# Expert weights fetched early by the sync engine, their high and low parts made in halves, one per tile

## The reference

```python
x = x + 0.5 * ffn(layernorm(x), Wg, W11, W12, W2)
x = x + attn(layernorm(x), ...)      # conv, two linear recurrences, gate
x = x + 0.5 * ffn(layernorm(x), Wg, W11, W12, W2)

def ffn(x, Wg, W11, W12, W2):        # 8 experts, the best 2 of each row
    scores = softmax(x @ Wg); top, idx = top_k(scores, 2); top /= top.sum() + 1e-8
    gate, value = x @ W11[e], x @ W12[e]            # 256 -> 512
    out_e = (gate * sigmoid(gate) * value) @ W2[e]  # 512 -> 256
    return sum of top * out_e over the two chosen e
```

## Time and profile before

| what | value |
|---|---|
| median of three runs | 1039.33 us |
| profiled execution | 1031.17 us, span 1029.4 us |
| PE busy | 919.6 us, 89% of the span |
| DVE, ACT, POOL busy | 600.6, 330.0, 602.4 us |
| round 0, first matmul of tile 0 to first matmul of tile 70 | 84.21 to 445.52 us |
| round 1, the same | 668.21 to 1008.30 us |
| DMA queues | q0 (POOL) 37.83 MB, q1 (SP) 49.82 MB, q10 (ACT) 23.61 MB |

### The profile page before, as it was taken

One profiled execution on the slowest core, in us unless ns is written; L12 is line 12 of the kernel. 1 busy time (PEld: TensorE's weight loads), 2 busy tenths in 40 slices (PEclk: granted clock), 3 DMA queues, 4 the chain that ended last, 5 costly groups with the idle time before them and its releaser, 6 DMA issues.

```text
span 1029.4 us, 20399 instructions
## 1 busy us (share of the span) xinstructions
PE 919.6 (89%) x5412; PEld 794.1 (77%) x5413; DVE 600.6 (58%) x1478; ACT 330.0 (32%) x655; POOL 602.4 (59%) x549
## 2 busy tenths in 40 slices
PE   7957999999999999984997995399999999999995
PEld 6945878888888888873775684388888888888884
DVE  5486656656556465536766885855555555555552
ACT  3431333424334332221226541023233223322321
POOL 4104766767667677743214770157777777777773
PEclk9999999999999999997999996599999999999998
DMA  9435466464573754323212547234344343343332
GB/s 345 141 103 185 77 173 159 81 191 108 139 190 57 195 131 92 57 27 108 62 41 61 185 143 317 89 87 73 58 78 68 57 78 55 72 76 58 52 49 30
DMA packets 75970, 111.86 MB, mean 109 GB/s; under 512 B 11792, under 2 KB 60816, under 8 KB 75600
## 3 DMA queue, kind: packets, MB, share of 16 engines
q0 software_dynamic: 31808, 37.83, 23.8%
q1 hardware_dynamic: 31744, 49.82, 14.3%
q10 hardware_dynamic: 12368, 23.61, 6.6%
HBM read 66.79 MB, written 48.63 MB: 112 GB/s over the span
## 4 chain that ended last, share of the span: by engine, by line
PE 66%; DVE 12%; DMA 6%; issue 5%; POOL 4%; ACTq 3%; ACT 3%; POOLq 0%; DVEq 0%; SPq 0%
PE bank L1254 34%; PE bank L1277 16%; PE bank L1263 5%; PE bank L1246 3%; DMA x_rows<-yb,idx_i 3%; PE bank L1182 2%; PE bank L1371 2%; DVE work L787 2%; DMA xn_rows<-work 1%; DVE bnst L775 1%; POOL seq L438 1%; DVE sg L947 1%; DVE work L861 1%; ACT sg L617 1%; DVE w_lo L1019 1%
## 5 line engine op out<-in xcount | busy, mean ns | idle before, releaser
L947 DVE TENSOR_TENSOR sg<-sg,bank 128x512 f32<-128x512 f32 x142 | 97.7, 688 | 303.3 <-ACT sg L617 303.3
L1254 PE MATMUL bank<-w_hi,xt_hi 128*128 x568 | 241.8, 426 | 17.8 <-DVE xt_lo L936 15.9
L1254 PE MATMUL bank<-w_hi,xt_lo 128*128 x568 | 225.3, 397 | 0.0
L1254 PE MATMUL bank<-w_lo,xt_hi 128*128 x568 | 223.6, 394 | 0.0
L449 POOL DMA_INDIRECT xg<-xn_rows,idx_i x142 | 144.3, 1016 | 116.4 <-DVE idx_i L875 73.8
L609 ACT ACTIVATE yb<-bank,gates_in 128x256 f32<-128x256 f32 x142 | 67.3, 474 | 448.6 <-DMA out_rows<-yb,idx_i 216.6
L453 POOL DMA_INDIRECT gates_in<-gate_rows,idx_g x142 | 136.4, 961 | 52.0 <-issue 41.7
L1277 PE MATMUL bank<-w_hi,ft_hi 128*128 x568 | 159.4, 281 | 7.2 <-ACT yb L609 7.2
L462 POOL DMA_INDIRECT x_rows<-yb,idx_i x71 | 115.4, 1626 | 77.1 <-DMA x_rows<-yb,idx_i 36.1
L1277 PE MATMUL bank<-w_hi,ft_lo 128*128 x568 | 160.1, 282 | 0.0
L1277 PE MATMUL bank<-w_lo,ft_hi 128*128 x568 | 159.9, 282 | 0.0
(11 more groups left out here) (209 smaller groups left out, 1249.5 us busy)
## 6 DMA issues: line engine op xcount, KB each, us to landing
xn_rows<-work SPq DMA_DIRECT2D x16, 512.0 KB, 2.8
w_lo_rows<-w_lo ACTq DMA_DIRECT2D x16, 512.0 KB
w_lo<-w_lo_rows SPq DMA_DIRECT2D x16, 512.0 KB
work<-x_rows SPq DMA_DIRECT2D x16, 512.0 KB, 3.7
w_lo<-w_lo_rows SPq DMA_DIRECT2D x2, 4096.0 KB, 17.8
x_all<-x SPq DMA_DIRECT2D x8, 512.0 KB, 8.2
w_lo_rows<-in_sb ACTq DMA_DIRECT2D x16, 256.0 KB, 2.4
out_rows<-seq SPq DMA_DIRECT2D x8, 512.0 KB, 3.3
```

The source lines that it names most:

```text
L947: nc.vector.tensor_tensor(sg[p], sg[p], ps_g[p][:], ALU.mult).then_inc(f_step, 1)
L1254: last = nc.tensor.matmul(dst[p][:], xt[p][:, c, :], of(w), start=(c == 0 and n == 0), stop=(c == DC - 1 and n == len(parts) - 1))
```

## The change

Four things change, all in round 0.

1. The loads of slots 1 to 7 leave ACT. SP issues them, one slot as soon as `ye_done` is at j+1, that is, behind `down(0)` for slot 1, behind `down(1)` for slot 2, up to `down(6)` for slot 7. W2 is loaded straight into its place in `w2_hi`, in one DMA of 512 KB.
2. ACT makes the high parts in pieces of 512 columns, one for each of the steps s = 1 to 6. For W2 a piece takes two instructions: raw values to `w2_stage`, a wait for that, and the rounded copy back.
3. DVE makes the low parts in pieces of 512 columns, at s = 2 to 7.
4. ACT stores only the low part of W2, in one DMA at s = 0 of the next group; the low parts of W11 and W12 are stored by SP, slot 0 behind the last load, slot j behind the load of W2's low part of slot j.

```diff
+        def load_down(q, j, e):
+            q.dma_start(w2_hi[:, j * IC:(j + 1) * IC, :].bitcast(F32), w2[...]...).then_inc(w2_in[j], 16)
+        def load_slot(q, j):
+            e = expert_of_slot(q, j)
+            load_up(q, j, e)
+            load_down(q, j, e)
...
             store_gates(0)
-            load_w2_lo(0)
+            load_w2_lo(0, 0)
+            for j in range(1, E):
+                sp.wait_ge(ye_done, j + 1)
+                load_slot(sp, j)
+            store_up_lo(0)
+            for j in range(1, E):
+                load_w2_lo(0, j)
+                store_up_lo(j)
+            sp.wait_ge(w2_lo_in, E * 16)
...
+            def high_up(j, c):
+                act.wait_ge(w11_in[j], 16)
+                nc.scalar.activation(w11_hi[:, j * DC + c, :], w11_raw[:, j * DC + c, :], ACT.Copy).then_inc(hi11_ready, 1)
...
+            def high_down(j, h):
+                at_ = w2_hi[:, j * IC + 2 * h:j * IC + 2 * h + 2, :].rearrange("p c d -> p (c d)")
+                act.wait_ge(w2_in[j], 16)
+                if j > 0:
+                    act.wait_ge(w2_lo_out, 16 * j)
+                nc.scalar.activation(w2_stage[h], at_.bitcast(F32), ACT.Copy).then_inc(staged, 1)
+                act.wait_ge(staged, 2 * j + h + 1)
+                nc.scalar.activation(at_, w2_stage[h], ACT.Copy).then_inc(hi2_ready, 1)
...
             def weights_step(t):
                 j, s = t // MIN_TILES + 1, t % MIN_TILES
                 if t == 0:
                     store_low(0)
                 if j < E:
-                    if s == 0:
-                        load_up(act, j, expert_of_slot(act, j))
-                    if s == 1:
-                        for h in range(2):
-                            act.wait_ge(w2_lo_out[h], 16 * j)
-                        load_down(act, expert_of_slot(act, j))
-                    if s == 3:
-                        high_up(j)
-                    if s == 4:
-                        high_value(j)
-                    if s == 5:
-                        high_down(j)
-                    if s == 7:
-                        store_low(j)
+                    if s in (1, 2):
+                        high_up(j, s - 1)
+                    if s in (3, 4):
+                        high_value(j, s - 3)
+                    if s in (5, 6):
+                        high_down(j, s - 5)
+                if s == 0 and 2 <= j <= E:
+                    store_low(j - 1)
...
@@ VectorE, weights_step @@
-                    if s == 4:
-                        low_up(j)
-                    if s == 5:
-                        low_value(j)
-                    if s == 6:
-                        low_down(j)
+                    if s in (2, 3):
+                        low_up(j, s - 2)
+                    if s in (4, 5):
+                        low_value(j, s - 4)
+                    if s in (6, 7):
+                        low_down(j, s - 6)
```

More of the change, by code:

```diff
@@ L217, in build @@
         s_cols, s_setw, s_wg, s_attw = (sem(n) for n in ("s_cols", "s_setw", "s_wg", "s_attw"))
-        s_w2 = [sem(f"s_w2_{b}") for b in range(2)]
+        w2_in, staged = [sem(f"w2_in{j}") for j in range(E)], sem("staged")
+        w11_in, w12_in = ([sem(f"{n}_{j}") for j in range(E)] for n in ("w11_in", "w12_in"))
         hi2_ready, lo2_ready, w2_lo_in = sem("hi2_ready"), sem("lo2_ready"), sem("w2_lo_in")
-        w2_lo_out = [sem(f"w2_lo_out{b}") for b in range(2)]
+        w2_lo_out = sem("w2_lo_out")
         tap_ready, m_done, m_step, m_ready, lo_step, xlo_ready = (sem(n) for n in ("tap_ready", "m_done", "m_step", "m_ready", "lo_step", "xlo_ready"))
@@ L318, in _, with load_w2_lo @@
-            store_gates(0)
-            load_w2_lo(0)
+            def load_w2_lo(r, j):
+                b = j % 2
+                if j == 0:
+                    sp.wait_ge(tiles_ready, r + 1)
+                if r == 0:
+                    sp.wait_ge(w2_lo_out, 16 * (j + 1))
+                if j >= 2:
+                    used = sp.value_load(tile_ends[0:1, j - 2:j - 1], min_val=0, max_val=ET) + (r * ET + 1)
+                    sp.wait_ge(ye_done, used)
+                if 16 * j + E * 16 * r > 0:
+                    sp.wait_ge(w2_lo_in, 16 * j + E * 16 * r)
+                sp.dma_start(w2_lo[:, b * IC:(b + 1) * IC, :].bitcast(F32).rearrange("p c d -> p (c d)"),
+                             w2_lo_dram[:, j * IC * D:(j + 1) * IC * D]).then_inc(w2_lo_in, 16)
@@ L364, in _ @@
             store_gates(1)
-            load_w2_lo(1)
+            for j in range(E):
+                load_w2_lo(1, j)
+            sp.wait_ge(w2_lo_in, E * 16 * 2)
             sp.wait_ge(pads_out, 48)
@@ L532, in load_table @@
                 nc.scalar.activation(table[:], ssm[:, ONE:ONE + 1], function)
[L534 to L544, removed]
@@ new lines, in high_value @@
+            def high_value(j, c):
+                act.wait_ge(w12_in[j], 16)
+                nc.scalar.activation(w12_hi[:, j * DC + c, :], w12_raw[:, j * DC + c, :], ACT.Copy).then_inc(hi12_ready, 1)
+            def high_down(j, h):
[6 more added lines that the diff above has]
+                nc.scalar.activation(at_, w2_stage[h], ACT.Copy).then_inc(hi2_ready, 1)
@@ L656, in _ @@
             router_exp(0)
-            high_up(0)
-            high_value(0)
-            high_down(0)
+            for high in (high_up, high_value, high_down):
+                for c in range(2):
+                    high(0, c)
             experts(0)
@@ L956, in experts @@
                 if r == 0:
-                    low_up(0)
-                    low_value(0)
+                    for c in range(DC):
+                        low_up(0, c)
+                    for c in range(DC):
+                        low_value(0, c)
                     dve.wait_ge(pads_out, 48)
                     rows_in(0, 0)
-                    low_down(0)
+                    for h in range(2):
+                        low_down(0, h)
                     gates(0)
```

78 lines of the change are left out of this document (23 added, 55 removed).

## The result

The changed kernel takes 1055.26 us (median of 4, 1053.95 to 1058.59), the kernel before on the same chip 1040.78 (1038.33 to 1042.59). The ratio is 1.0135, its 95% interval 1.0101 to 1.017: slower by 1.35%. The prediction was 1036.3, with 1043 as its upper end.

A forecast was written before the change was run, and what follows sets the result against it. ACT's steps were taken to cause round 0's stalls: 22.5 us over plain tiles would become 0.6 + 0.5 + 4.8 + 7.3 + 1.0 + 4.5 + 1.0 = 19.7. So 1039.3 - 3 = 1036.3 us, range 1029 to 1043.

The forecast's parts named there:

- The stalls of before are ACT's: Round 0 of the kernel before: ACT's steps delay PE, most of 22.5 us that are not matmul work.
- ACT's pieces: Round 0, ACT: 512-column pieces cost 0.5 us in steps 1 to 4 and 4.8 us in steps 5 and 6.
- the 0.7: Steps 5 and 6 on ACT: two dependent instructions each, costing PE 0.7 us a group, 4.8 us in seven groups.
- register reads: ACT's two reads ahead of each `yb`: 1.0 us allowed for those beside a store, bounds 0 and 3.
- The wait of tile 2: Tile 2, once: `sg(2)` queues behind ACT's wait for slot 1's W11, so tile 3 starts 7.3 us later, bounds 6.8 and 8.5.
- The 0.8: Part of tile 2's wait: 0.8 us from the end of `down(0)` to SP's first load of slot 1.
- The low clock: Behind tile 2's gap: PE restarts at a lower granted clock, 1.0 us, between 0 and 1.7.
- The bunch: Slots 2 to 7 loaded at ends of tiles 3 to 8: scatters every 6.4 us, 4.5 us of stall on PE.
- rival B: Scatter chain holds PE while loads last: interval 7.4 over seven scatters, 13.8 instead of 4.5, result 1045.6; chance 0.12.
- the room of 0.61: ACT's spare time before `sg` delays PE's next tile: 0.61 us, so a 0.52 us piece costs nothing.
- the waits in front: Waits ahead of ACT's pieces in steps 1 to 4: 0.5 us over 28 steps, bounds 0 and 2.5.
- rival C: Pieces of steps 1 to 4 don't fit, or register reads are slow throughout: 5 us more, 1041; chance 0.11.

The follow-up runs named there:

- e10: The kernel before with the gate gathers of tiles 4 to 70 left out in round 0 (values wrong, only time read): 1038.31 us.
- e14: e3 with one more wait, which puts the stores of low W11 and W12 of slots 1 to 7 behind tiles further on: 1025.86 us, ratio 0.9941.
- e11: The changed kernel with the gate gathers of tiles 4 to 70 left out in round 0 (values wrong, only time read): 1048.9 us.
- e2: The changed kernel with slots 2 to 7 loaded one per group of eight tiles, slot 1 still late: 1046.95 us.
- e4: The changed kernel with a slot loaded at every second tile instead of every tile: 1043.26 us.
- e1: The changed kernel with slot 1 loaded right behind slot 0, ahead of round 0: 1038.15 us.
- e12: The changed kernel as it is, run and profiled again: 1053.37 us, ratio 1.0136.
- e3: The changed kernel with slot 1 loaded right behind slot 0 and the other slots one per group: 1036.0 us, ratio 1.0016.
- e8: e3 with W2's high part made by one instruction in steps 5 and 6, and W2's low part left out: 1044.64 us.
- e15: e13 with the stores of low W11 and W12 three tiles behind the low W2: 1029.99 us, ratio 0.9982.
- e13: e3 with the loads of slots 2 to 7 issued by ACT again: 1032.65 us, ratio 0.9993.
- e9: e3 with the gate gathers of tiles 4 to 70 left out in round 0 (values wrong, only time read): 1037.59 us.

## Why the prediction was wrong, step by step

1. **The stalls of before are ACT's: right.** None of its tiles has the mark of the chain, and with less work for POOL (e10) the stalls stay (25.7); 3.3 a group.
2. **ACT's pieces: right in mechanism, a little low.** Steps 1 to 4 fit: in the first three groups of e14 the tiles behind them take 4.82 to 4.94 (tile 3: 5.00). Behind steps 5 and 6 tiles take 5.40 and 4.94, 0.66 together, as the 0.7 said. A group without a late `yb` loses 0.9 to 1.4 (e14, e11), forecast 0.9 with register reads.
3. **The wait of tile 2: right, sized 1.6 low.** Forecast 7.3, bounds 6.8 and 8.5; measured 8.9. The terms 3.5, 0.52 and 2.35 were met (100.82 to 104.14, 104.68, 107.02). The 0.8 from the end of `down(0)` to SP's load measured 2.4: 1.66 of it pass before SP's next instruction. No row names what held SP; the queue of instruction loads, q8, has no packet between 92 and 102 us. In e2 and e4, whose code on SP differs, the same gap is 0.03 us, and tile 2 takes 12.37 and 12.23, a wait of 7.5 and 7.4. e1 takes the wait away whole. The low clock cost 1.4 (2.8 in e12), forecast 1.0.
4. **The bunch: the step that failed first and most.** "An interval of 6.4 us between the calm 4.77 and the 7.49: (6.4 - 4.86) x 5.5 scatters - 4.0 = 4.5 us of stall". The interval was 7.9 for six scatters: by the same formula (7.9 - 4.86) x 6 - 4.0 = 14.2, measured 16.5 in tiles 6 to 11, of which 0.6 is ACT's. So the formula and the slack give most of it, and the interval was the term that failed. It was chosen below both rows shown beside traffic, 7.28 and 7.49, because I expected quick scatters in between. With the DMAs at a share of 0.92 for 50 us the quickest of the six intervals was 5.82, and the longest 11.71. That e2, which takes the bunch away, loses 1.4 us in these tiles shows that it is the bunch. This is rival B, to which I gave 0.12, and even its 13.8 was low. The reason against it, that a stall thins the loads, did not hold it under that.
5. **Missing: `yb` late without the chain, a second step that failed.** Groups 2 to 6 lose 2.3 us on average, forecast 0.9; that is the second large term, 7.1 us. The prediction took `yb` to start at the same place in every tile, 1.5 us behind PE's, so that a piece of 0.52 fits into the room of 0.61, and put the waits in front at 0.5 us for all 28 steps. In seven of these 40 tiles it starts 0.5 to 1.5 us later, not held by a scatter (see e12), and they lose 6.5 us. It is nearest to rival C. The cause is open; it goes with POOL's gate gathers, since e11 has none of it.
6. **Missing: what lets the chain catch up. This is why undoing both faults gained nothing.** I wrote that one bunch a group "eats nearly that much and is made up later, so it is hidden now". That is so in the kernel before: no tile there has the mark. But the chain makes up only some 0.2 us a tile by itself, because a scatter takes 4.6 to land. In the kernel before a group's eight tiles are 3.3 us longer through ACT's steps, and the chain gets these too: 1.9 + 3.3 = 5.2 us of credit. Shorten ACT's steps and the credit shrinks with the stalls: the marked tiles hold nothing in the kernel before, 18.4 us in e3, and 27.2 in e8, where ACT's steps are shorter still. That it is this credit, and not another effect of where the traffic stands, is argued from these three and not tested by itself.

As to the whole, the 18.8 us that round 0 grew by: 10.3 for tiles 2 and 3, and 13.5 for tiles 6 to 11 (16.5, where the kernel before has 3.0), less 4.7 in groups 2 to 6 (11.7 instead of 16.4); 0.3 less is left for the rest. Each undone alone (e1, e2) brings a part back, both (e3) only the kernel before, and e14, which also keeps the traffic of a group apart, gains 0.6%. Why 1.5 MB in one go hold up the scatters more than 0.5 and 1.0 MB apart isn't settled. That it is so is shown by e14 against e3, one wait apart; e15 against e13 points the same way. Whether it is the gap itself or the stores' new place in the tile no run separates.

## What to carry to other kernels

A chain of dependent transfers that takes nearly as long as a tile has almost no way to catch up: find its quiet interval, the tile and the slack, and take the interval under load from the nearest loaded rows, not from between them and the quiet ones. A stall on another engine may be what pays for that chain, so that removing the stall gains nothing until the chain is relieved as well. And before a stall is put down to the chain, look in the rows whether the engine went on right behind a landing: in the changed kernel it did so in the bunch and nowhere else. Traffic that no one waits for has a place too: one wait more on the queue that issues it was worth more here than the whole reordering.

## What the runs showed of the hardware

- A scatter with addition of 128 rows of 1 KB takes 4.6 us from one issue to the next, when each waits for the landing of the one before, and it is the same with two gathers issued in between as with one (medians of 4.64 in e3 and e9). It takes 5.4 to 10.9 us to land while 512 KB transfers keep another queue busy.
- Its first packet comes 2.1 to 2.2 us behind its start on POOL in quiet, and 2.1 to 5.3 beside such transfers. From 131.5 to 134.5 SP's queue had the 16 engines to itself, at 1.13 MB, with a scatter issued and not landed.
- SP went on 1.66 us behind the end of the matmul that it waited for (1.77 and 1.83 in e12 and e11), where it was 0.03 us in e2 and e4; the cause isn't known.
- A register read on ACT, 0.28 us as a median, took 1.55 at 156.35 in the changed kernel, beside such transfers.
